# Differential attention: VectorE's third addition behind the maxima of the fifth batch, the normalising product behind those of the sixth

## What is computed

```python
Q1, Q2 = (Q[..., :hd], Q[..., hd:])
K1, K2 = (K[..., :hd], K[..., hd:])
attn1 = softmax(einsum('bhnd,bhmd->bhnm', Q1, K1) * scale, axis=-1)
attn2 = softmax(einsum('bhnd,bhmd->bhnm', Q2, K2) * scale, axis=-1)
out = einsum('bhnm,bhmd->bhnd', attn1 - lam * attn2, V)
```

## Time and profile before

| what | value |
|---|---|
| time, median of three runs (lowest to highest) | 5336.15 us (5335.23 to 5339.29) |
| time of the profiled execution | 5341.33 us |
| its span, first to last instruction | 5339.6 us |
| TensorE busy, share of the span | 4968.2 us, 93% |
| VectorE, ScalarE, GpSimd busy | 3456.5, 2365.5, 2878.0 us |
| mean granted TensorE clock over the span | 0.962 |
| third additions of VectorE in the stage (L617 into `sum_dve`) | 96, mean 2217 ns |
| normalising products (L633) | 96, 559 to 1770 ns, median 948 ns |

### The profile page before, as it was taken

How to read it: one execution, slowest core, us unless ns; L and a number is a source line. 1 busy time by engine, 2 the same in 40 slices (tenths; PEclk the granted TensorE clock), 3 DMA queues, 4 the chain that set the end, 5 groups by cost and what they waited for, 6 DMA issues and landing times. The chain is left out here.

```text
span 5339.6 us, 68289 instructions
## 1 busy us (share of the span) xinstructions
PE 4968.2 (93%) x23988; PEld 3051.7 (57%) x23988; DVE 3456.5 (65%) x5195; ACT 2365.5 (44%) x5309; POOL 2878.0 (54%) x1506
## 2 busy tenths in 40 slices
PE   8799999999999999999999699699996988988699
PEld 4466666666666666666666344477764555555355
DVE  3478788888878888878878355555544444454484
ACT  3255555555555555555555322144442333333332
POOL 0089889889899889988888511166670000000000
PEclk9899999999999999999999788799997999999999
DMA  6611111111111111111110355512201000000101
GB/s 224 212 41 43 26 39 47 44 30 40 40 46 41 34 32 46 47 30 37 40 47 13 80 162 162 148 44 55 68 16 63 24 24 13 17 18 12 55 4 54
DMA packets 230078, 295.91 MB, mean 55 GB/s; under 512 B 83518, under 2 KB 213254, under 8 KB 222222
## 3 DMA queue, kind: packets, MB, share of 16 engines
q1 hardware_dynamic: 229776, 292.06, 19.7%
HBM read 178.11 MB, written 113.87 MB: 55 GB/s over the span
## 5 line engine op out<-in xcount | busy, mean ns | idle before, releaser
L671 POOL TENSOR_TENSOR diff_run_pool<-diff_run_pool,diff_probs 128x768 f32<-128x768 f32 x1056 | 2099.6, 1988 | 233.7 <-ACT diff_probs L514 107.2
L594 DVE TENSOR_REDUCE diff_maxes<-diff_max 128x1 f32<-128x512 f32 (+1 forms) x2880 | 1620.4, 628 | 456.0 <-PE diff_max L430 455.8
L514 ACT ACTIVATE diff_probs<-diff_ring 128x384 f32<-128x384 f32 x3456 | 1389.4, 508 | 846.8 <-PE diff_ring L419 805.0
L455 PE MATMUL diff_out_ps<-diff_probs,diff_vs 128*64 128x384 f32 x6912 | 1241.6, 494 | 0.0
L430 PE MATMUL diff_max<-diff_ks,diff_qs 96*128 96x512 f32 (+1 forms) x2880 | 1164.5, 406 | 42.1 <-DMA diff_ks<-qk_hi 29.4
L419 PE MATMUL diff_ring<-diff_qs,diff_ks 97*128 97x384 f32 x3456 | 986.5, 340 | 1.3 <-ACT diff_qs L521 0.4
L430 PEld LDWEIGHTS diff_max<-diff_ks,diff_qs 96*128 96x128 f32 x2880 | 546.5, 190 | 435.2 <-issue 341.7
L455 PEld LDWEIGHTS diff_out_ps<-diff_probs,diff_vs 128*64 128x64 f32 x6912 | 444.8, 136 | 505.6 <-issue 290.3
L419 PEld LDWEIGHTS diff_ring<-diff_qs,diff_ks 97*128 97x128 f32 x3456 | 654.0, 189 | 98.0 <-ACT diff_probs L514 6.1
L2048 POOL MEMSET ffn_before<- 128x128 f32 x1 | 0.2, 204 | 987.9 <-POOLq L63 987.9
L1312 DVE TENSOR_REDUCE causal_maxes<-causal_max 128x2 f32<-128x768 f32 (+2 forms) x252 | 219.9, 873 | 250.7 <-PE causal_max L1187 167.4
(11 more groups left out here) (230 smaller groups left out, 5933.1 us busy)
## 6 DMA issues: line engine op xcount, KB each, us to landing
qk_hi<-proj_hi SPq DMA_DIRECT2D x12, 1536.0 KB, 5.8
qk_lo<-proj_lo SPq DMA_DIRECT2D x12, 1536.0 KB, 9.6
diff_qs<-qk_hi SPq DMA_DIRECT2D x64, 288.0 KB, 4.3
diff_ks<-qk_hi SPq DMA_DIRECT2D x64, 288.0 KB, 6.1
diff_recip<-row_factors SPq DMA_DIRECT2D x192, 96.0 KB, 2.8
o_rows<-diff_normed SPq DMA_DIRECT2D x96, 192.0 KB, 1.9
v_rows<-proj_vst SPq DMA_DIRECT2D x12, 768.0 KB, 7.6
diff_qs<-qk_lo SPq DMA_DIRECT2D x32, 288.0 KB, 5.3
```

What stands on the lines that cost most here:

```text
L455: mm = pe.matmul(out_ps[VD * j:VD * (j + 1), 0:w], vs[n % 2][:, g, j, :], probs[g % PBUF][:, j, 0:w], start=g == 0, stop=g == STEPS - 1, t ...
L514: act.activation(probs[g % PBUF][:, j, 0:w], ring[at % BANKS][:, 0:w], ACT.Exp, scale=SCALE).then_inc(s_taken, 1)
L594: dve.tensor_reduce(maxes[q % 2][:, j, s:s + 1, h], max_ps[u % MAX_BANKS][:, 0:w], AX.X, ALU.max).then_inc(s_red, 1)
L671: pool.tensor_tensor(to[:, :, 0:w], acc[:, :, 0:w], probs[g % PBUF][:, :, 0:w], ALU.add).then_inc(s_accp, 1)
```

## The change

Two numbers that place VectorE's instructions:

```diff
-    SUMS_AT, ROWS_AT, COMPACT_AT, NORMAL_AT = 1, 4, 2, 4
+    SUMS_AT, ROWS_AT, COMPACT_AT, NORMAL_AT = 1, 4, 2, 5
...
-    add_after = {1: 1, 3: 2, 5: 3}
+    add_after = {1: 1, 3: 2, 4: 3}
```

## The result

The changed kernel took 5292.79 us (median of 4 runs, 5290.97 to 5299.81), the kernel before 5335.69 on the same chip: a ratio of 0.9924, 95% interval 0.9912 to 0.9936, or 43 us less. Measured once more it took 5297.74 us (5 runs, 5293.63 to 5303.45) against 5334.39, ratio 0.9932 (0.9918 to 0.9945), 37 us less. The profiled execution took 5293.17 us and spans 5291.4.

What follows compares the result with a forecast made beforehand. TensorE was taken as the bound, its batch 0 delayed by VectorE's reductions, late because GpSimd holds the third addition. Terms -33 + 1 + 3 = -29 us off the 5336.15 median gave 5307 us, range 5298 to 5345.

Steps and rivals of the forecast that it cites:

- The mechanism: VectorE instructions with two SBUF inputs are held by GpSimd additions; swapping the two places brings batch 0 from 4.84 to 4.40 us.
- a choice between two rows: VectorE additions: one 0.10 us before GpSimd's start got in, one 0.04 after was held; the product's 0.07 before gets in.
- The sum's first two terms: Differential attention: -33 us from 0.44 us in batch 0 of 76 chunks, and +1 us for the 20 other chunks.
- the heads' ends: The 20 other chunks: GpSimd starts late, the product is held, ScalarE's outputs' copy is 0.24 us late; 1 us, bound 5.
- The loads: SyncE's queue: next head's loads, behind the later store, overlap the sums by 0.1 us in 15 chunks; +3 us, 0 to 17.
- The range's low end: Whole kernel: 5298 us, for no collision between loads and sums and a few more than 76 chunks gaining.
- The lost race: Rival: GpSimd gets in before the product, delaying ScalarE's outputs' copy and batch 0; +36 us, 5372 (5360 to 5390); 18%.
- the mixture: Rival: a third of the 76 chunks lose the product's race with GpSimd; 5330 us (5320 to 5345); 10%.
- The collisions: Rival: next head's loads delay the sums in all 15 chunks while the product gets in; +17, 5321 us; 8%.
- the change of hands: Product against GpSimd's addition: the start time where the winner switches, between 0.10 us before and 0.04 after GpSimd's start.

Runs made afterwards that it cites:

- loads_first: Next head's loads put ahead of the product's store in SyncE's order, against the changed kernel; 5298.68 us, ratio 0.9928 to the kernel before.
- after: The changed kernel itself, first measurement, against the kernel before; 5292.79 us, ratio 0.9924.
- after_again: The changed kernel, unaltered, measured once more against the kernel before; 5297.74 us, ratio 0.9932.
- act_scale_before: The kernel before with the scaling of the next head's values moved from VectorE to ScalarE; 5326.68 us, ratio 0.9983 to the kernel before.
- late2: Two tiny VectorE reciprocals put ahead of each product, against the changed kernel; 5360.46 us, ratio 1.0045 to the kernel before.
- late1: One tiny VectorE reciprocal put ahead of each product, against the changed kernel; 5298.90 us, ratio 0.9932 to the kernel before.
- early: Product issued ahead of batch 5's fourth maximum instead of behind the fifth, against the changed kernel; 5296.80 us, ratio 0.9928 to the kernel before.
- add_only: Only the third addition moved, behind batch 4 with the product kept there, against the kernel before; 5412.80 us, ratio 1.0145.
- norm_only: Only the product moved, behind batch 5 where the third addition stays, against the kernel before; 5685.05 us, ratio 1.0655.

## Where the prediction held, and the step that failed

**The mechanism** held in each step, for the two instructions that moved. The third addition was put at about 1.35 us and has a median of 1.350; the product at 0.56 and has 0.547; its start at 0.07 us ahead of GpSimd, and it was 0.06 in the chunk shown; GpSimd's addition behind it at some 2.2, and it takes 2.17. Batch 0 came to 4.39, forecast 4.40. That the product gets in was a choice between two rows, with a small margin: one chunk was lost at 0.036 us behind, one won at 0.002 ahead.

**The sum's first two terms**, -33 for batch 0 and +1 for the heads' ends, make -32; batch 0's mean gives -32.1. The product was held in the heads' ends as forecast (1.47 us in most of them) and made ScalarE wait 15 times. TensorE's reserve covered that everywhere but at 355.74, the lost race, which made that batch 0 last 5.09 us, 0.7 too long.

**The loads** were forecast to meet the sums by 0.1 us, and do by 0.2. The +3 for it, out of 0 to 17, was too much: 0 to 1.5 by the late additions, and loads_first, which takes the overlap away, gains nothing.

**The step that failed** is the list of terms in the sum: it has none for the scaling of the next head's values (L587), and so takes batch 3's change as nothing. The runs showed -5.5 us there in after and -9.7 in after_again. The prediction followed the later GpSimd to its race with the product and no further; but what moves GpSimd in batch 5 moves it in batch 2 of the next chunk as well, past the scaling that it had been holding. The instruction stands in the streams shown ahead of the prediction, with its place unchanged, and was given no cost. That its hold is what made batch 3 long, act_scale_before shows: with the scaling on ScalarE the excess is 1.9 us, from 16.8. With -5.5 in place of +3 the sum is -37.5, attention's -37.4.

**The range's low end**, 5298, had no room for either: neither for a second instruction that is held less, nor for the spread of the later stages. The two medians of the same kernel, 5292.79 and 5297.74, lie 5 us apart, and both lie below 5298, the second by 0.3; 5336.15 - 37.5 = 5298.7 is near the second. The 10 us that the profiled rest of the kernel got shorter (2325.4 to 2315.5) are not shown to be a gain of the change: the profiled execution of before was itself 5 us above its median, and after_again's rest is 2320.6. Where the first median's last 5 us come from stays open.

**The rivals.** The lost race did not come, but late2 shows it some 0.15 us away, near its price. Of the mixture one chunk came true. The collisions were met and cost next to nothing.

By the Trainium skill, SBUF — State Buffer, section Who interferes with whom, the instruction that issues first keeps the shared pair and the other blocks: the rows at 327.93 and 355.74 agree. By the Trainium skill, Perfetto Trace Analysis, section GPSIMD Engine Instruction, a GpSimd span in a profile is to be treated as unreliable. At the scale of this race that holds in part: in the 64 chunks in which the changed kernel's product starts 0.03 to 0.08 us ahead of GpSimd's recorded start, it got in 64 times, but in late1 it also got in in the 55 chunks in which it starts 0.01 to 0.05 us behind.

## What to carry to other kernels

Where two engines hold each other, place the instruction by the other engine's rhythm: either well inside its operation with idle time behind (early), or clearly ahead of its next start, and measure the margin, since here some 0.15 us more would have turned a gain of 40 us into a loss of 26. After moving one instruction, follow the other engine's shift through a whole period and look at every instruction that it meets, not only the two that were moved. An instruction that waits for a transfer belongs behind the work that doesn't need it: that alone was worth another 11 to 16 us.

## What the hardware showed that was not expected

- Two VectorE instructions with two SBUF inputs, back to back, don't keep out a GpSimd addition that waits: the second VectorE instruction takes 2.18 us (add_only).
- Behind one and the same instruction the change of hands is sharp: in late1 the product got in 0.052 us behind GpSimd's start, at 0.057 it was held, and the difference is 0.51 against 2.18 us. From one kind of instruction to the next it moves. In early a scaling recorded 0.02 us ahead of GpSimd was held, 2.46 us:

```profile
1606.54 2.46 DVE L587 TENSOR_SCALAR diff_vs<-diff_vs,diff_neg_lam 128x1152 f32<-128x1152 f32 x1
```
```profile
1606.56 1.82 POOL L674 TENSOR_TENSOR diff_run_pool<-diff_run_pool,diff_probs 128x768 f32<-128x768 f32 x1
```

- The scaling, with one large input of 128x1152 and a scalar for each partition, is held like an addition: 0.80 us alone, a median of 2.28 in the kernel before.
- In norm_only a wait of 2.46 us of TensorE was followed by the 1.2 GHz level (granted clock 0.50) and matmuls of 0.65 and 0.63 us in place of 0.34 and 0.40; over the stage that is an estimated loss of 159 us, worked out above.
